# Causal attention with a mixture of experts: gates, routing and dispatch moved from a preamble into the attention heads, two tiles at a time

## The reference, cut to what matters

```
x  = L0_attn_x                      # (4, 1024, 256) f32
xn = layernorm(x)
out = x + attention(xn) + ffn(xn)

attention: 16 heads of 128. q = (xn @ Wq + bq).reshape(b, h, t, dh)  (no transpose:
           a head's queries come from 64 tokens), k and v per head from all 1024 tokens,
           causal softmax(q k / sqrt(128)) @ v, then @ Wo + bo
ffn:       su = xn @ w_shared_up; y, g = split(su); shared = (silu(g) * y) @ w_shared_down
           scores = sigmoid(xn @ w_gate)          # 64 experts
           topk_idx = top_k(scores, 6); w = scores of the six / their sum
           pos = running count of each expert over all tokens in order; valid = pos < 128
           x_disp[e, pos] = xn of the token
           out_r = (silu(g_r) * v_r) @ w_down  with g_r, v_r = split(x_disp @ w_up)
           routed = sum over the six of w * out_r[e, pos] (0 where not valid)
           ffn = shared + routed
```

## Time and profile before

| what | value |
|---|---|
| median of 3 runs | 1989.14 us (1989.06 to 1991.62) |
| the profiled execution, own time | 1983.72 us |
| its span | 1982.0 us |
| PE / DVE / ACT / POOL busy | 1654.8 / 1536.1 / 1091.1 / 1107.3 us |
| instructions | 49196 |
| DMA moved | 253.35 MB, mean 128 GB/s |

### The profile page before, as it was taken

How to read it: one execution, slowest core, us unless ns; L and a number is a source line. 1 busy time by engine, 2 the same in 40 slices (tenths; PEclk the granted TensorE clock), 3 DMA queues, 4 the chain that set the end, 5 groups by cost and what they waited for, 6 DMA issues and landing times. The chain is left out here.

```text
span 1982.0 us, 49196 instructions
## 1 busy us (share of the span) xinstructions
PE 1654.8 (83%) x19015; PEld 1293.7 (65%) x19016; DVE 1536.1 (78%) x3148; ACT 1091.1 (55%) x2300; POOL 1107.3 (56%) x920
## 2 busy tenths in 40 slices
PE   1243069999999999999967799999999999999997
PEld 1242047777777777777756677766666766776775
DVE  5589967777777777777744469988898988889885
ACT  1531046666666666666632256655656655665664
POOL 0420037777777777777730056667666666666643
PEclk9677589999999999999987699999999999999999
DMA  6325047777757766766667657777777787678655
GB/s 190 106 85 225 0 105 145 141 142 141 125 113 113 130 110 107 108 108 108 109 135 220 180 116 129 126 135 145 133 128 122 128 148 128 129 125 150 121 97 109
DMA packets 695996, 253.35 MB, mean 128 GB/s; under 512 B 642384, under 2 KB 682145, under 8 KB 695008
## 3 DMA queue, kind: packets, MB, share of 16 engines
q1 hardware_dynamic: 668096, 204.12, 55.7%
q0 software_dynamic: 19232, 37.84, 7.7%
q10 hardware_dynamic: 8448, 8.39, 1.2%
HBM read 61.30 MB, written 54.66 MB: 59 GB/s over the span
## 5 line engine op out<-in xcount | busy, mean ns | idle before, releaser
L448 POOL TENSOR_TENSOR prob<-prob 128x128 f16<-128x128 f32 (+7 forms) x512 | 654.6, 1283 | 722.4 <-ACT prob L790 716.8
L783 ACT ACTIVATE prob<-prob,nmax 128x128 f32<-128x128 f32 (+7 forms) x512 | 397.4, 776 | 534.2 <-DVE prob L1142 534.2
L607 PE MATMUL ps_s<-kT,qT 128*128 128x512 f16 (+3 forms) x2304 | 457.0, 326 | 2.4 <-DVE kT L1129 1.2
L622 PE MATMUL ps_o<-probT,vh 128*128 128x256 f16 (+1 forms) x3840 | 423.9, 263 | 3.8 <-DMA probT<-prob 3.8
L1142 DVE TENSOR_SCALAR_CACHE_REDUCE prob<-ps_s,neg_scale 128x128 f32<-128x128 f32 (+7 forms) x512 | 409.3, 809 | 7.9 <-PE ps_s L609 7.9
L622 PEld LDWEIGHTS ps_o<-probT,vh 128*128 128x128 f16 x3840 | 366.7, 98 | 47.2 <-issue 4.3
L790 ACT CAST prob<-prob 128x128 f16<-128x128 f32 (+7 forms) x512 | 340.9, 666 | 2.3
L607 PEld LDWEIGHTS ps_s<-kT,qT 128*128 128x128 f16 x2304 | 201.9, 98 | 148.7 <-issue 4.2
L633 PE MATMUL ps_y<-wo,oT 128*128 128x256 f16 x1536 | 211.5, 274 | 85.2 <-DVE oT L1157 85.2
L567 PE MATMUL ps_t<-xT,wq 128*128 128x64 f16 x6144 | 203.1, 194 | 66.4 <-DMA xT<-xn_columns 61.0
L567 PEld LDWEIGHTS ps_t<-xT,wq 128*128 128x128 f16 x6144 | 191.5, 99 | 75.9 <-issue 61.8
(11 more groups left out here) (182 smaller groups left out, 1752.3 us busy)
## 6 DMA issues: line engine op xcount, KB each, us to landing
dispatched<-zeros SPq DMA_DIRECT2D x16, 512.0 KB, 5.4
probT<-prob SPq DMA_TRANSPOSE x512
ex<-dispatched SPq DMA_DIRECT2D x16, 512.0 KB, 4.5
expert_out<-eo ACTq DMA_DIRECT2D x16, 512.0 KB, 3.8
resid<-in_L_attn_x_dram SPq DMA_DIRECT2D x2, 2048.0 KB, 11.1
xn_rows<-xn SPq DMA_DIRECT2D x8, 512.0 KB, 3.0
xn_columns<-xnth SPq DMA_DIRECT2D x16, 256.0 KB, 2.3
xT<-xn_columns SPq DMA_DIRECT2D x8, 512.0 KB, 5.8
```

Of the source, the lines that this page charges most:

```text
L448: pool.tensor_tensor(low_cols(j), prob_cols(j).rearrange("p (r k) -> p r k", k=P), high_cols(j), ALU.subtract).then_inc(p_low, 1)
L607: pe.matmul(s_cols(j, lo, hi), qT[:, u, a, j * P:(j + 1) * P], kT[:, u, c, lo:hi], start=(n == 0), stop=(n == 2 and hi < w))
L622: mm = pe.matmul(ps_o[:, lo:2 * P], vh[:, u, a, r * D:(r + 1) * D], probT[:, PT_AT[c] + 2 * r + s, lo:], start=(r + n == 0), stop=(r == 2 ...
L783: nc.scalar.activation(prob_cols(j), prob_cols(j), ACT.Exp, bias=nmax[:, j:j + 1], scale=-1.0, accum_out=rsum[:, i % 2, j:j + 1]).then_inc ...
```

## The change

**Preamble.** Only what head 0 needs: 1 MB of x (batch 0), normalised into `xn0`, transposed (16 transposes) and split straight from PSUM into `xT`, and the four weights. All four have staging buffers of their own (`stg[0..3]`, 64 KB a partition, under what the heads use later). DVE makes the low halves of wq, wk and wv in one operation each from the unscaled staging (`low_weights`); only wo keeps the scaled copy on ACT and the subtraction on POOL. The other 3 MB of x come last. `xn_rows` holds batch 0 alone. The zero fill of `dispatched` is issued on SP before the heads, and the first row load waits for it.

**Behind the heads.** The 32 tiles are taken as 16 pairs p; pair p has heads 2p (even part) and 2p + 1 (odd part), with a late part in head 2p + 2. They use the two `ps_t` banks between the projections.
- Even: POOL normalises two tiles (for p < 4, SP loads them instead), PE transposes them after `project_k(i + 1, 0)`, ACT copies (and for p >= 4 casts, DVE makes the low half, SP stores the columns), PE multiplies by the gate and shared weights after `project_k(i + 1, 1)`.
- Odd: ACT copies the gates, DVE takes logits, top values and indices, compares (`choose`, 768 columns), `shared_hidden` in three steps, POOL adds the masks, PE transposes the hidden and counts slots (`count_slots`), DVE makes slots and overflow, POOL multiplies (`pick`), PE does `shared_down`. The running count over tiles is kept in `slot_base`.
- Late: DVE adds the shared expert to `resid` and sums the slots.

Scatters begin at head 2, and the split moves from 32 to 34 heads. Statistics of the other 24 tiles run on DVE in heads 0 to 7, their square root on ACT in head 7. `xT` has one buffer: at heads 15, 31 and 47 (`turn`) v comes before the next q, and SP reloads xT in two parts. The query's high and low splits are as before.

The diff, cut to its core (memory and semaphore declarations left out):

```diff
-        SPLIT = B * H // 2
+        NP = NT // 2
+        ROWS = 2 * NP
+        SPLIT = ROWS + 2
+        GATES = E + 2 * HS
         PASSES = ((0, 0), (0, 1), (1, 0))
+
+        def even_part(i):
+            return i // 2 if i % 2 == 0 and i < ROWS else -1
+
+        def odd_part(i):
+            return i // 2 if i % 2 == 1 and i < ROWS else -1
+
+        def late_part(i):
+            return i // 2 - 1 if i % 2 == 0 and 2 <= i <= ROWS else -1
+
+        def turn(i, more):
+            return more and i % H == H - 1
...
+            sp.dma_start(resid[:, 0:TB, :], x_v[:, 0:TB, :]).then_inc(x_in[0], 16)
+            for n in range(2):
+                sp.dma_start(stg[n][:].rearrange("p (k n) -> p k n", k=KC), views[n]).then_inc(wload[n], 16)
+            sp.dma_start(bqT[:], bq.rearrange("(m d) -> d m", d=D)).then_inc(w_in, 16)
+            sp.dma_start(bkT[:], bk.rearrange("(m d) -> d m", d=D)).then_inc(w_in, 16)
+            for n in range(2, 4):
+                sp.dma_start(stg[n][:].rearrange("p (k n) -> p k n", k=(KC, H)[n - 2]), views[n]).then_inc(wload[n], 16)
+            sp.dma_start(bvT[:], bv.rearrange("(m d) -> d m", d=D)).then_inc(w_in, 16)
+            sp.dma_start(cvec[:], bo.partition_broadcast(P)).then_inc(w_in, 16)
             sp.dma_start(w_gs[:, :, 0:E], w_gate.rearrange("(k p) n -> p k n", p=P)).then_inc(w_in, 16)
             sp.dma_start(w_gs[:, :, E:], w_sup.rearrange("(k p) n -> p k n", p=P)).then_inc(w_in, 16)
             for n in range(2):
-                sp.dma_start(stg[n].rearrange("p (k n) -> p k n", k=KC), views[n]).then_inc(wload[n], 16)
-            for n in range(2):
                 sp.dma_start(w_sd[n * HS:(n + 1) * HS, :], w_sdown).then_inc(w_in, 16)
-            sp.dma_start(bqT[:], bq.rearrange("(m d) -> d m", d=D)).then_inc(w_in, 16)
-            sp.dma_start(bkT[:], bk.rearrange("(m d) -> d m", d=D)).then_inc(w_in, 16)
-            sp.dma_start(bvT[:], bv.rearrange("(m d) -> d m", d=D)).then_inc(w_in, 16)
-            sp.dma_start(cvec[:], bo.partition_broadcast(P)).then_inc(w_in, 16)
-            with sp.Fori(0, NG) as g:
-                sp.wait_ge(xn_ready, G4 * g + G4)
-                sp.dma_start(xn_d.rearrange("(t p) c -> p t c", p=P)[:, bass.ds(g * G4, G4), :], xn[:]).then_inc(xn_stored, 16)
-                sp.wait_ge(xn_low, KC * g + KC)
-                for n in range(2):
-                    sp.dma_start(xnT_d[:, n, :, bass.ds(g * (G4 * P), G4 * P)], xnth[:, n, :, :]).then_inc(xt_stored, 16)
-
+            sp.dma_start(resid[:, TB:, :], x_v[:, TB:, :]).then_inc(x_in[1], 16)
+            sp.wait_ge(xn0_ready, TB)
+            sp.dma_start(xn_d, xn0[:]).then_inc(xn0_stored, 16)
...
             def load_xT(b):
-                if b > 1:
-                    sp.wait_ge(v_done, 2 * H * (b - 1))
+                sp.wait_ge(xt_stored, 32 * NC * b)
+                sp.wait_ge(v_done, 2 * H * b)
                 for n in range(2):
-                    sp.dma_start(xT[:, b % 2, n, :, :], xnT_d[:, n, :, b * T:(b + 1) * T]).then_inc(xT_in[b % 2], 16)
-
-            def load_rows(t):
-                if t > 1:
-                    sp.wait_ge(scattered[t % 2], 16 * TOPK * (t // 2))
-                sp.dma_start(stage_x[:, t % 2, :], xn_d[t * P:(t + 1) * P, :]).then_inc(stage_in[t % 2], 16)
+                    sp.dma_start(xT[:, n, :, 0:TPH], xnT_d[:, n, :, b * T:b * T + TPH]).then_inc(xT_head, 16)
+                for n in range(2):
+                    sp.dma_start(xT[:, n, :, TPH:], xnT_d[:, n, :, b * T + TPH:(b + 1) * T]).then_inc(xT_in, 16)
...
+                        if j == 1 and turn(i, i < B * H - 1):
+                            load_xT(i // H + 1)
...
+            pool.wait_ge(whigh, 5)
+            pool.tensor_tensor(wo[:, 1, :, :].rearrange("p a b -> p (a b)"), stg[3][:],
+                               wo[:, 0, :, :].rearrange("p a b -> p (a b)"), ALU.subtract).then_inc(wsplit[3], 1)
...
+            def pick(p):
+                pool.wait_ge(slot_step, 3 * p + 3)
+                pool.tensor_tensor(picked[:], chosen[:], slots_e[:].unsqueeze(2).to_broadcast([P, 2, TOPK, E]), ALU.mult).then_inc(picked_ready, 1)
...
+            def gates(i, p):
+                if p == 0:
+                    pe.wait_ge(w_in, W_IN)
+                pe.wait_ge(k_low, 2 * (i + 1) + 1)
+                pe.wait_ge(bt_copy, p + 1)
+                for t in range(2):
+                    for k in range(KC):
+                        mm = pe.matmul(ps_t[:, 0, t * GATES:(t + 1) * GATES], xnt[:, k, t * P:(t + 1) * P],
+                                       w_gs[:, k, :], start=(k == 0), stop=(k == KC - 1))
+                mm.then_inc(bg_done, 1)
+
+            def count_slots(i, p):
+                free_second_bank(i)
+                pe.wait_ge(sh_ready, p + 1)
+                pe.transpose(ps_t[:, 1, 0:P], sh[:].rearrange("p t h -> p (t h)"), ident[:])
+                pe.wait_ge(mask_step, 3 * p + 3)
+                flat = mask[:].rearrange("p t e -> p (t e)")
+                pe.matmul(ps_t[:, 1, P:P + 2 * E], tri[:], flat, start=True, stop=False)
+                pe.matmul(ps_t[:, 1, P + E:P + 2 * E], ones[:], mask[:, 0, :], start=False, stop=True)
+                pe.matmul(ps_t[:, 1, P + 2 * E:P + 3 * E], ones[:], mask[:, 0, :], start=True, stop=False)
+                pe.matmul(ps_t[:, 1, P + 2 * E:P + 3 * E], ones[:], mask[:, 1, :], start=False, stop=True).then_inc(bh_done, 1)
+
+            def shared_down(i, p):
+                pe.wait_ge(k_low, 2 * (i + 1) + 1)
+                pe.wait_ge(bh_copy, p + 1)
+                for t in range(2):
+                    rows = slice(t * HS, (t + 1) * HS)
+                    mm = pe.matmul(ps_t[:, 0, t * C:(t + 1) * C], hsT[rows, :], w_sd[rows, :], start=True, stop=True)
+                    if t == 0:
+                        mm.then_inc(bd_half, 1)
+                        pe.wait_ge(bd_half, p + 1)
+                mm.then_inc(bd_done, 1)
...
+            act.wait_ge(cvec_done, 1)
+            nc.scalar.activation(stg[3][:], stg[3][:], ACT.Copy, scale=scales[:, 3:4]).then_inc(whigh, 1)
...
+            def low_weights(n):
+                w = (wq, wk, wv)[n]
+                dve.wait_ge(whigh, n + 1)
+                V.scalar_tensor_tensor(w[:, 1, :, :].rearrange("p a b -> p (a b)"), stg[n][:], scales[:, n:n + 1],
+                                       w[:, 0, :, :].rearrange("p a b -> p (a b)"), ALU.mult, ALU.subtract).then_inc(wsplit[n], 1)
...
+                    swap, even, odd, late = turn(i, more), even_part(i), odd_part(i), late_part(i)
                     block_max(i, 0)
                     low_q(i, 1)
                     mix_at(0)
                     low_k(i, 1)
+                    if odd >= 0:
+                        take_logits(odd)
+                    if late >= 0:
+                        add_shared(late, NC * (i - 1))
                     if old:
                         invert_sums(i - 1)
                     mix_at(1)
@@ -1210,31 +1346,61 @@
                         add_y(i - 1, 0, mixed(1))
                         low_o(i - 1, 1)
                     block_max(i, 1)
-                    if more:
+                    if odd >= 0:
+                        top_values(odd)
+                    if late >= 0:
+                        slot_indices(late)
+                    if i0 == 0 and i < TB:
+                        later_stats(i)
+                    if odd >= 0:
+                        top_indices(odd)
+                        choose(odd)
+                    if swap:
+                        low_v(i, 0)
+                        low_v(i, 1)
+                    elif more:
                         full_q(i + 1, 0)
                         full_q(i + 1, 1)
                     mix_at(2)
                     block_max(i, 2)
                     mix_at(3)
+                    if odd >= 0:
+                        shared_hidden(odd, 0)
                     if old:
                         low_o(i - 1, 2)
                         add_y(i - 1, 1, mixed(3))
                     block_max(i, 3)
                     mix_at(4)
-                    if more:
-                        low_q(i + 1, 0)
-                    low_v(i, 0)
-                    low_v(i, 1)
+                    if odd >= 0:
+                        shared_hidden(odd, 1)
+                    if swap:
+                        full_q(i + 1, 0)
+                        full_q(i + 1, 1)
+                    else:
+                        if more:
+                            low_q(i + 1, 0)
+                        low_v(i, 0)
+                        low_v(i, 1)
+                    if odd >= 0:
+                        shared_hidden(odd, 2)
                     block_max(i, 4)
                     mix_at(5)
                     if old:
                         add_y(i - 1, 2, mixed(5))
                         low_o(i - 1, 3)
                     block_max(i, 5)
+                    if swap:
+                        low_q(i + 1, 0)
```

(6 more changed lines are left out.)

904 lines of the change are left out of this document (505 added, 399 removed).

## The result

The changed kernel takes 1938.72 us (median of 4 runs, 1934.47 to 1939.58), beside 1989.41 for the kernel before on the same chip: ratio 0.974 (95% interval 0.973 to 0.975), or 51 us less. The forecast was 84 us less. The profiled execution took 1938.18 us, with a span of 1936.4; before these were 1983.72 and 1982.0, so the spans differ by 45.6 us. Ratios use executions in the chip's fast state; the one slow execution of all (2299.78 us, in experiment 12) is in no ratio, but it is among the four whose median is given there.

What follows compares the result with a forecast made beforehand. PE was taken to bound the first stage's heads, with some added DVE work free. 1983.7 - 180.1 (preamble) + 85 (pairs) + 6 + 5 (once only) = 1899.6, with 5.4 added 1905 us; range 1880 to 1930, all cases 1858 to 1950.

Steps and rivals of the forecast that it cites:

- rival B: Heads: POOL blocks DVE harder, 0.85 us on average, and lateness carries over; 8 us a pair, 1948 us; chance 0.2.
- Part 1: Preamble: the first low_q ends at 89.6 us instead of 269.74, a gain of 180.1 us (170 to 190).
- the lock at the end: Preamble's end: DVE's first low_q waits for POOL's whole split of wo, ending at 89.6 us, not 82.3.
- Part 2: First stage: heads take in sixteen pairs of tiles at 5.3 us per pair, 85 us in all.
- exchange rate: Heads: about 3.0 us of added DVE work per head is free, the rest is paid; taken from the second stage.
- Yscale in even heads: First stage: behind add_shared, yscale loses its 0.1 us margin to POOL's subtraction; 1.9 us, near 2.1 long.
- Odd head longer than even: First stage, a sign to look for: odd head pays 3.5 us by DVE work, even head 1.3.
- Once only: Heads 0 to 7: 24 statistics and a root, 6 us; xT reloads at three heads, 1.7 each, 5 us.
- Part 3: Experts and mixing: no cost; two unmixed heads change stage, gate weights hide under the first expert load.
- A: Heads: DVE's added work fits, only PE's work is paid, 2.4 us a pair; 1858 us; chance 0.2.
- C: Heads: five DVE operations and yscale blocked by whole POOL operations in each pair, 12.8 us; 2025 us; chance 0.03.
- D: Preamble: first row load waits for zeros 20 us late, delaying head 0's transposes; 1925 us; chance 0.02.

Runs made afterwards that it cites:

- experiment 12: Also `before_early`: kernel before the change, with yscale right after the second low_q and slot 1's mixing step later; 1958.72 us, ratio 0.986.
- Experiment 3: Changed kernel with POOL's split of wo in eight operations of 512 columns instead of one of 4096; 1931.93 us, ratio 0.974.
- bank_first: Also run 1: changed kernel with DVE's take_logits and add_shared moved ahead of low_q and low_k; 1949.95 us, ratio 0.983.
- slots_late: `bank_first` with the even heads' slot_indices moved behind full_q; 1923.20 us, ratio 0.969.
- run 5: The same kernel as `slots_late`: `bank_first` with slot_indices of even heads behind full_q; 1923.20 us, ratio 0.969.
- orders: Changed kernel with banks emptied first, slot_indices behind full_q, yscale early and wo split in eight pieces; 1880.12 us, ratio 0.947.
- run 9: Changed kernel with the gate matmuls of each pair run twice on PE; 1936.22 us, ratio 0.976.
- run 10: The same kernel as `compare_twice`: changed kernel with DVE's comparison computed twice in odd heads; 1954.95 us, ratio 0.985.
- experiment 6: Changed kernel with yscale right after the second low_q and slot 1's mixing step behind the first add_y and low_o; 1912.99 us, ratio 0.964.
- compare_twice: Changed kernel with DVE's 768-column comparison computed twice in odd heads; 1954.95 us, ratio 0.985.

## Why the prediction was right and where it was off

**Bound and direction: right.** The preamble left the path for 180.3 us, and the first stage took 121 us of it back, 107 of them by the sixteen pairs. The measured median, 1938.72, lies inside the whole range (1858 to 1950), but outside the forecast's own (1880 to 1930) and nearer to rival B's 1948 than to the forecast's 1905. That it is inside is owed to the room left for a rival.

**Part 1: right in each step.** The scaling of loads by bytes (35 us for 35.56), the weights' chain (70.0 for 69.99) and the lock at the end (8 us long, end at 89.5) all stand. Experiment 3 shows the lock's 7 us to be real and mostly avoidable: the first low_q ends 6.3 us earlier.

**Part 2 is the step that failed, and it failed twice over.** First by sizes, which nearly cancelled. PE's gates were taken from the earlier trace rows as 16 matmuls in 2.84 us. Groups of the changed kernel:

```profile
L654 PE MATMUL ps_t<-w_gs,xnt 128*128 128x192 f32 x8 | 1.5, 326 | 0.0
...
L674 PE MATMUL ps_t<-w_sd,hsT 64*128 64x256 f32 x4 | 1.4, 428 | 0.1
...
L1193 DVE TENSOR_TENSOR chosen<-iota_e,i8f 128x768 bf16<-128x768 f32 x1 | 1.1, 1083 | 0.1
...
L1189 DVE CAST i8f<-i 128x16 f32<-128x16 uint32 x1 | 0.2, 176 | 0.0
L1230 DVE TENSOR_SCALAR slot_idx<-i8f 128x12 uint32<-128x12 f32 x1 | 0.2, 174 | 0.0
```

Four f32 gate matmuls a pair leave eight rows: an f32 matmul shows as two. So the x16 of the earlier trace rows were 8 matmuls of 0.36 us, and the gates cost 1.46 us (0.71 forecast), the down product 1.45 (0.76): PE got 3.4 us, not 2.4. DVE was taken too dear: its odd head is busy 22.67 us, the even one 21.03, beside 17.6 before, so 5.0 and 3.4 more where 6.5 and 4.1 were forecast. Most of that is the 2.0 us for blocks by POOL: the comparison takes 1.08 us for 0.96 at its shortest, the overflow test 0.46 for 0.29, the products 0.28 and 0.29, so blocks came to about 0.3 us. By the Trainium skill's rule on copies and tensor_scalar, which the prediction cites (SBUF — State Buffer, "Who interferes with whom"), cast and clamp would have cost more still; in this kernel both take 0.17 us in every pair. That goes with the order and is no property of the cast: in `bank_first` and `slots_late` the same cast takes up to 1.19 us, which agrees with that rule. Groups of `slots_late`:

```profile
L1189 DVE CAST i8f<-i 128x16 f32<-128x16 uint32 x16 | 11.8, 740 | 0.5
```

Why it is blocked there and not here is open. The clamp is never blocked in these three kernels.

Second, and this is what decided, by the **exchange rate**. "About 3.0 us of added DVE work per head is free" came from the mixing steps of the second stage, which stand in other places of DVE's queue. With the right sizes it would give 5.0 - 3.0 = 2.0 for the odd head, 1.9 for the even one (PE's own added work, 25.18 - 23.24) and 0.7 for half of PE's work in the odd one: 4.6 us a pair. Measured were 6.7. What runs 5 and 1 show in its place: the new work holds the bank that the next projection needs, and what counts is how late in its queue DVE reaches it. Put first and with the wait for POOL behind `full_q`, the same work costs 6.0 us a pair on average, and 5.0 where the cast is not blocked (5.0 on average in `orders`); put as in the change, 6.7; put first with the wait ahead of `full_q`, 6.6 to 8.3, 7.5 on average. Runs 9 and 10 show how unlike the places are: 1.3 us more on PE ahead of a late bank cost nothing, 1.7 us more on DVE ahead of `full_q` cost 1.7. There is no one rate at which DVE's work is free.

**The place of the wait: wrong.** I looked for 2 to 3 us before ps_y, released by oT. The amount was right, 2.9 us, but the place is `project_q`, released by `add_shared` and `take_logits`. **Yscale in even heads** is blocked as said, 1.64 us for about 2, but experiment 6 shows that nothing hangs on it in this stage; the 1.9 us put down for it were free. **Odd head longer than even: wrong.** Each mark falls behind the wait at `project_q`, so the even head's interval carries the odd head's wait (1.76) and the other way round (1.17), and PE is busy 0.4 us longer in the even head (25.18 for 24.74).

**Once only.** Heads 1 to 8, with the later statistics, cost 8.2 us above later pairs (6 forecast); the reload of xT costs 2.5 us a turn (1.7 forecast).

**Part 3: "nothing" was off by 12 us.** 8.1 are in the experts, whose code is unchanged. Busy time in the part where they start, the kernel before and then the changed one:

```profile
1030.00:1045.00 15.00, 10.62 (x71) 9.39 (x72) 6.28 (x13) 3.43 (x8) 0.00 (x0) 0.73 0.83 216
```

```profile
1019.00:1034.00 15.00, 11.68 (x58) 11.11 (x62) 4.91 (x10) 2.19 (x6) 0.00 (x0) 0.50 0.75 190
```

The granted clock in these 15 us is 0.50 instead of 0.73; over the whole stretch it is 0.72 instead of 0.75. From kernel to kernel the stretch takes 159.0 to 167.1 us, in `before_early` 161.5, and no edit of mine aimed at it; why the clock is lower there stays open. The other 3.9 us are in the second stage and the tail; 1.6 of them lie in one head, two behind the turn at head 47 (27.45 us for 25.88), with a mean granted clock of 0.94.

**The sum.** Against the profiled executions I was 38.6 us too low (1899.6 for 1938.2): 23 from the pairs, about 4 from statistics and turns, 8 from the experts, 4 from the second stage. The 5.4 us between median and profiled execution did not recur (0.5), which leaves 34 of the median.

**Rivals.** A (DVE's work fits) fell: PE's waits for DVE are 2.9 us a pair. It comes nearest in `orders`, where the pair is 5.0 us longer and 3.6 of that are PE's work. B (8 us, through harder blocks) fell for this kernel, since the blocks are small. In `bank_first` the size comes about in the pairs with a blocked cast (7.9 to 8.3 us), partly by B's own mechanism and partly by the wait for POOL's result. C and D did not occur.

## What to carry to other kernels

When work is pushed into an in-order queue, don't price it by its length alone: ask which buffer it holds, who wants that buffer next, and what it has to wait for itself. Work that frees a shared bank goes first, work that waits for another engine goes behind whatever a busy engine is waiting for; three such moves and one split of a long operation brought 2.8% here, where the change as it stood brought 2.6%; about half of the 2.8% is the early yscale in the second stage, which the kernel before could have had as well. Length still counts at places that everything later in the head hangs on: a second comparison ahead of `full_q` was paid in full. A rate of free work taken from one stage holds only for work at the same places of the queue.

## What the runs showed of the hardware that I had not expected

- **A wait of PE can be followed by half clock (0.50, which is 1.2 GHz; 1.00 is 2.4), but the same wait need not be.** In `compare_twice` PE waits 2.04 us for `add_shared` in nearly every pair. Behind some of these waits the granted clock is 0.50 for about 3 us, behind others it stays at 1.00; the changed kernel has waits of 2.04 us in four early heads, all followed by 1.00, and one of 1.88 us (at 468 us) followed by 0.50. Busy time behind two equal waits of `compare_twice`:

```profile
588.10:591.10 3.00, 3.00 (x98) 2.93 (x99) 2.91 (x5) 0.26 (x2) 2.81 (x3) 1.00 0.53 98
753.32:756.32 3.00, 3.00 (x78) 3.00 (x79) 2.91 (x5) 0.26 (x2) 2.81 (x3) 0.73 0.54 99
```

  What decides is open. It costs little where PE has waits left to fill: 0.1 us a pair in `compare_twice`, 0.35 in an even head of `bank_first`. It costs more at a reload of xT: in the changed kernel the 3.13 us at 505 us were followed by 1.00, while 5.07 us at the same turn in `orders` were followed by half clock. Timeline of PE in `orders` at that turn, and busy time of the stretch behind it:

```profile
485.71 5.30 PE L585 MATMUL ps_t<-xT,wq 128*128 128x64 f16 x96 [5.07 <-DMA xT<-xn_columns]
```

```profile
487.00:490.00 3.00, 3.00 (x61) 3.00 (x59) 1.02 (x1) 0.00 (x0) 1.24 (x2) 0.50 1.16 300
```

  The 96 matmuls take 5.30 us there, 2.97 at full clock. That turn therefore costs 6.5 us (32.09 against 25.58), twice the 3.2 of the changed kernel, and over the run PE waits 14.1 us for xT in `orders`, 7.6 in the changed kernel.
- **The lock of DVE and POOL also hits a tensor_scalar of 8 columns** (up to 2.20 us), and in experiment 3 it lasts as long as the POOL instruction in flight: with eight short ones in place of a long one DVE got through in 1.25 us. A cast of 16 columns can be hit too: 1.18 us for 0.17 in `slots_late`. That one, from 808.47 to 809.65 us, outlasts POOL's scatter issue (808.15 to 809.15) and meets the subtraction begun at 809.17, so one POOL instruction is no general bound.
- **An f32 matmul leaves two rows in the trace** where an f16 one leaves one; a count of rows is not a count of matmuls.
